# Retention stage of a two-layer transformer kernel: all four score groups at once, a chunk pipeline one step deeper, and GpSimd weighting the gathered expert rows

## The reference

```python
# end of layer 0: each token adds its two experts' rows, weighted
weighted = fc2 * padded_probs[:, None]
moe_out = jnp.zeros((N, H)).at[padded_tid].add(weighted)
x = h1 + moe_out
# layer 1, retention: 8 sequences of 512 tokens, 16 heads of 16
y = layernorm(x)
Q, K, V = y @ WQ, y @ WK, y @ WV          # per head
Q, K = xpos_rotate(Q), xpos_rotate(K)
R = ((Q @ K^T) * decay_mask) @ V          # causal, one decay per head
x = x + group_norm(R, gamma, beta) @ WO
```

## Time and profile before

| | us |
|---|---|
| median of three runs | 2053.84 (2051.27 to 2053.95) |
| the profiled execution | 2054.74 |
| its span, from the first to the last instruction | 2053.0 |
| retention stage in it | about 1425 to 1780 |

### The profile page before, as it was taken

How to read it: one execution, slowest core, us unless ns; L and a number is a source line. 1 busy time by engine, 2 the same in 40 slices (tenths; PEclk the granted TensorE clock), 3 DMA queues, 4 the chain that set the end, 5 groups by cost and what they waited for, 6 DMA issues and landing times. The chain is left out here.

```text
span 2053.0 us, 33292 instructions
## 1 busy us (share of the span) xinstructions
PE 1724.3 (84%) x10092; PEld 1280.7 (62%) x10092; DVE 1209.3 (59%) x3206; ACT 667.7 (33%) x2056; POOL 583.1 (28%) x668
## 2 busy tenths in 40 slices
PE   4767766999899967267857999996899999799998
PEld 2444435777677744156756888885566666456655
DVE  5999994777677765799843221222677777422221
ACT  2545554554455424012320111111344444211111
POOL 2434432000000011787516333332344443200000
PEclk9998987999999989678865999998999999799999
DMA  6000000000000000000022324222000000000000
GB/s 184 19 13 15 15 18 11 11 11 12 13 11 12 1 9 0 6 3 21 34 95 67 93 85 110 92 86 98 27 27 26 26 26 26 1 11 20 10 20 21
DMA packets 55111, 71.08 MB, mean 35 GB/s; under 512 B 7074, under 2 KB 44898, under 8 KB 54626
## 3 DMA queue, kind: packets, MB, share of 16 engines
q1 hardware_dynamic: 37218, 40.46, 6.3%
q0 software_dynamic: 6912, 18.88, 3.6%
q10 hardware_dynamic: 10880, 10.49, 1.5%
HBM read 46.61 MB, written 23.20 MB: 34 GB/s over the span
## 5 line engine op out<-in xcount | busy, mean ns | idle before, releaser
L801 ACT ACTIVATE probs<-psS,nm 128x256 f32<-128x256 f32 x256 | 118.9, 469 | 189.5 <-DVE nm L834 189.5
L409 PE MATMUL psKV<-wkv,XT 128*128 128x512 f32 x256 | 135.8, 679 | 52.2 <-DVE acc L545 32.5
L1576 DVE COPY YE<-e_psY 128x512 f32<-128x512 f32 x40 | 27.7, 691 | 220.6 <-PE e_psY L1522 220.6
L545 DVE SCALAR_TENSOR_TENSOR acc<-psKV,G,acc 128x128 f32<-128x128 f32 x544 | 150.2, 333 | 6.7 <-ACT gated L470 6.7
L1512 PE MATMUL e_psH<-e_XT,w 128*128 128x256 f32 x640 | 147.1, 384 | 0.0
L1522 PE MATMUL e_psY<-w,e_HT 128*128 128x256 f32 x640 | 144.0, 379 | 0.0
L832 DVE TENSOR_REDUCE mx<-psS 128x2 f32<-128x512 f32 x128 | 87.9, 686 | 90.9 <-PE psS L722 90.9
L722 PE MATMUL psS<-Rec,QT 128*128 128x256 f32 (+1 forms) x512 | 133.7, 384 | 5.4 <-issue 4.5
L1482 POOL DMA_INDIRECT XE<-token_rows,held x80 | 76.0, 950 | 200.2 <-PE e_psX L1499 180.5
L1522 PEld LDWEIGHTS e_psY<-w,e_HT 128*128 128x128 f32 x640 | 121.6, 190 | 16.5
L1512 PEld LDWEIGHTS e_psH<-e_XT,w 128*128 128x128 f32 x640 | 120.6, 193 | 15.4
(11 more groups left out here) (254 smaller groups left out, 3872.0 us busy)
## 6 DMA issues: line engine op xcount, KB each, us to landing
expert_out<-YE ACTq DMA_DIRECT2D x40, 256.0 KB, 2.2
w<-in_w SPq DMA_DIRECT2D x16, 512.0 KB, 4.3
X<-in_x SPq DMA_DIRECT2D x8, 512.0 KB, 7.6
x_turned<-XT SPq DMA_DIRECT2D x32, 128.0 KB, 2.1
XS<-x_turned SPq DMA_DIRECT2D x8, 512.0 KB, 4.0
token_rows<-o_XN SPq DMA_DIRECT2D x32, 128.0 KB, 1.7
out_x<-X SPq DMA_DIRECT2D x8, 512.0 KB, 2.9
QT<-in_sel SPq DMA_DIRECT2D x2, 1024.0 KB, 11.5
```

Source lines behind the costliest of these rows:

```text
L409: mm = pe.matmul(psKV[v % 2][half][:, :, :], XT[:, v, c, :], wkv[:, c, half * 512:(half + 1) * 512], start=(c == 0), stop=(c == KC - 1))
L545: ins = nc.vector.scalar_tensor_tensor(acc[:, v % 2, e, :], kv, g, acc[:, v % 2, e, :], ALU.mult, ALU.add)
L801: nc.scalar.activation(probs[:, b.q % 4, hg, :], psS[b.q % 2][:, hg, :], ACT.Exp, bias=nm[:, b.q % 2, hg:hg + 1], scale=scale, accum_out=s ...
```

## The change

It leaves every stage but `retention` as it is. In `retention`:

- **Scores** are one piece: all four groups of 32 rows at once, into four banks of PSUM (`psS[r]`) where there were two. To make room, `psX` and `psV` share a bank (`psXV`), `psR`, the state's `psNew` and the turned inverses share one (`psRS`), and the variances go to `psQK`. Waits are added for that: to_state waits for result_read, variances for rotate of the entering chunk, inverses_turned for the state, project_v for the next chunk's x_turned.
- **The pipeline** has one more step: a step enters g, scores g-1, takes from_chunk, to_state, squared and variances of g-2, and lets g-3 leave. The rows of g+3 are gathered, those of g+2 are added and take their statistics, and g+1 is normalised and transposed. Steps -3 to 34 run where -2 to 33 did.
- **The expert rows** of a chunk are weighted and summed on GpSimd (`arrived` there: one multiply of 512 columns, one add of 256), behind the gather of the next chunk; VectorE adds only their sum to `X`.
- **Copies by parity** of V are a piece of their own on ScalarE (`values_parted`), read from `V` in SBUF.

```diff
--- before.py
+++ after.py
...
         cidx = k.sb(ctx, "cidx", [P, 2, 2], U32)
+        weight = k.sb(ctx, "weight", [P, 2, 2])
+        rows = k.sb(ctx, "n_rows", [P, 2, D])
...
-        psT = k.ps(ctx, "n_psT", [P, 2, KC, P])
+        psXV = k.ps(ctx, "n_psXV", [P, 2, D])
         psQK = k.ps(ctx, "n_psQK", [P, 2 * D])
-        psV = k.ps(ctx, "n_psV", [P, 2 * D])[:, 0:D]
         psK = k.ps(ctx, "n_psK", [P, 2, KC, P])
-        psX = k.ps(ctx, "n_psX", [P, 2, KC, P])
-        psVar, psInv = psX[:, 0, 0, 0:H1], psX[:, 1, :, :]
-        psS = [k.ps(ctx, f"n_psS{s}", [P, KC, 2, P]) for s in range(2)]
-        psR = k.ps(ctx, "n_psR", [P, 2, KC, P])[:, 0, :, :]
+        psRS = k.ps(ctx, "n_psRS", [P, 2, KC, P])
+        psS = [k.ps(ctx, f"n_psS{r}", [P, KC, 2, P]) for r in range(4)]
+        psX, psV = psXV[:, 0, :].rearrange("p (c t) -> p c t", c=KC), psXV[:, 1, :]
+        psR, psNew = psRS[:, 0, :, :], psRS[:, 1, :, :]
+        psInv, psVar = psR, psQK[:, 0:H1]
...
-            for g in range(-2, TS):
...
             with eng.Fori(1, NB - 1) as i:
                 for s in range(TS):
                     step(i, s, lambda d: True)
-            for g in range(NT - TS, NT + 2):
+            for g in range(NT - TS, NT + 3):
...
+        class Chunk:
+            def __init__(self, i, s, lag):
+                w = s + lag
+                self.g, self.i, self.s, self.x = i * TS + w, i + w // TS, w % TS, w % 2
+                self.pair = i * (TS // 2) + w // 2
+                self.states = self.i * (TS - 1) + self.s
+                self.adds = self.i * (TS - 2) + max(self.s - 1, 0)
+                self.ends = self.s == TS - 1
...
+            def turn_x(c):
+                pe.wait_ge(xn_ready, c.g + 1 + 2)
+                pe.wait_ge(z_added, c.g)
+                pe.wait_ge(v_evac, c.g)
...
+            def project_v(c):
+                pe.wait_ge(xt_evac, upto(c.g + 2))
+                pe.wait_ge(z_added, c.g + 1)
...
-            def scores(g, half):
-                if half == 0:
...
+            def scores(c):
+                pe.wait_ge(x_evac, c.g * 2 + 4)
+                pe.wait_ge(s_masked, c.g * 4 + 4)
+                for h in range(KC):
                     for par in range(2):
                         for r in range(4):
...
+            def to_state(c):
+                pe.wait_ge(r_read, c.g + 2)
...
+            def variances(c):
+                pe.wait_ge(sq_ready, c.g + 1)
+                pe.wait_ge(rot_done, upto(c.g + 3) + 1)
...
+            def inverses_turned(c):
+                pe.wait_ge(inv_spread, c.g + 1)
+                pe.wait_ge(st_done, c.g + 3)
...
             def step(i, s, has):
-                g, entering, attending, leaving = i * TS + s, has(0), has(-1), has(-2)
-                if attending:
-                    scores(g - 1, 0)
-                if leaving:
-                    variances(g - 2)
-                if entering:
-                    turn_x(g, s)
-                if attending:
-                    from_state(g - 1)
-                if entering:
-                    project_qk(g)
-                if leaving:
-                    inverses_turned(g - 2)
-                if entering:
-                    project_v(g)
-                if attending:
-                    scores(g - 1, 1)
-                if leaving:
-                    out(g - 2, entering)
-                if entering:
-                    turn_qk(g, s)
-                if attending:
-                    from_chunk(g - 1, s)
-                if attending and s != 0:
-                    to_state(s)
+                new, one, two, three = Chunk(i, s, 0), Chunk(i, s, -1), Chunk(i, s, -2), Chunk(i, s, -3)
+                if has(-3):
+                    inverses_turned(three)
+                if has(0):
+                    project_qk(new)
+                if has(-3):
+                    out(three)
+                if has(-2):
+                    from_state(two)
+                    from_chunk(two)
+                if has(-1):
+                    scores(one)
+                if has(-2):
+                    if not two.ends:
+                        to_state(two)
+                    variances(two)
+                if has(1):
+                    turn_x(Chunk(i, s, 1))
+                if has(0):
+                    turn_qk(new)
+                    project_v(new)
...
             def step(i, s, has):
-                g, entering, attending, leaving = i * TS + s, has(0), has(-1), has(-2)
-                if leaving:
-                    root_of(g - 2)
-                if entering:
-                    x_turned(g)
-                if leaving:
-                    inverse_spread(g - 2)
-                    scaled(g - 2)
-                if entering:
-                    values(g, s)
+                new, one, two, three = Chunk(i, s, 0), Chunk(i, s, -1), Chunk(i, s, -2), Chunk(i, s, -3)
+                if has(-3):
+                    scaled(three)
+                if has(-1):
+                    queries_turned(one)
+                    values_parted(one)
+                if has(2):
+                    deviation(Chunk(i, s, 2))
+                if has(-2):
+                    result_read(two)
+                    root_of(two)
                 if has(1):
-                    deviation(g + 1, (s + 1) % 2)
-                if entering:
-                    qk_turned(g)
-                if attending:
-                    result_read(g - 1, s)
+                    x_turned(Chunk(i, s, 1))
+                if has(-2):
+                    inverse_spread(two)
+                if has(0):
+                    keys_turned(new)
+                    values(new)
             stream(act, step)
...
-            def gathered(g, x, i):
-                pool.wait_ge(rows_used, g + 1)
-                nc.gpsimd.tensor_copy(cidx[:, x, :], k.slots[:, bass.ds(g, 1), :].rearrange("p a j -> p (a j)")).then_inc(i_ready, 1)
-                pool.wait_ge(i_ready, g + 1)
...
+            def gathered(c):
+                pool.wait_ge(first_added, c.g - 1) if not isinstance(c.g, int) or c.g > 1 else None
+                nc.gpsimd.tensor_copy(cidx[:, c.x, :], row(k.slots, c.g)).then_inc(i_ready, 1)
+                nc.gpsimd.tensor_copy(weight[:, c.x, :], row(k.prob, c.g)).then_inc(i_ready, 1)
+                pool.wait_ge(i_ready, c.g * 2 + 2)
                 pass_gate(k, pool)
                 for j in range(2):
-                    pool.indirect_dma_start(YG[:, x, j, :], None, k.y_dram[:, :],
-                                            bass.IndirectOffsetOnAxis(ap=cidx[:, x, j:j + 1], axis=0)).then_inc(got[x], 16)
...
+            def arrived(c):
+                pool.wait_ge(got[c.x], c.pair * 32 + 32)
+                pool.wait_ge(rows_used, c.g + 1)
+                nc.gpsimd.tensor_tensor(YG[:, c.x, :, :], YG[:, c.x, :, :], bc(weight[:, c.x, :].unsqueeze(2), [P, 2, D]),
+                                        ALU.mult).then_inc(weighed, 1)
+                pool.wait_ge(weighed, c.g + 1)
+                nc.gpsimd.tensor_tensor(rows[:, c.x, :], YG[:, c.x, 0, :], YG[:, c.x, 1, :], ALU.add).then_inc(first_added, 1)
...
             def step(i, s, has):
-                g, entering, attending, leaving = i * TS + s, has(0), has(-1), has(-2)
+                if has(3):
+                    gathered(Chunk(i, s, 3))
                 if has(2):
-                    gathered(g + 2, s % 2, i)
-                if entering:
-                    rotated(g, s)
-                if attending:
-                    squared(g - 1, s)
+                    arrived(Chunk(i, s, 2))
+                if has(0):
+                    rotated(Chunk(i, s, 0))
+                if has(-2):
+                    squared(Chunk(i, s, -2))
...
-            def arrived(g, x, pair, j):
-                if j == 0:
-                    dve.wait_ge(got[x], pair * 32 + 32)
-                else:
-                    dve.wait_ge(first_added, g + 1)
-                ins = nc.vector.scalar_tensor_tensor(row(k.X, g), YG[:, x, j, :], row(k.prob, g)[:, j:j + 1], row(k.X, g),
-                                                     ALU.mult, ALU.add)
-                ins.then_inc(rows_used if j else first_added, 1)
...
+            def arrived(c):
+                dve.wait_ge(first_added, c.g + 1)
...
+                nc.vector.tensor_tensor(row(k.X, c.g), row(k.X, c.g), rows[:, c.x, :], ALU.add).then_inc(rows_used, 1)
...
             def step(i, s, has):
-                g, entering, attending, leaving = i * TS + s, has(0), has(-1), has(-2)
-                if attending:
-                    mask(g - 1, 0)
-                if leaving:
-                    inverses(g - 2)
+                new, one, two, three = Chunk(i, s, 0), Chunk(i, s, -1), Chunk(i, s, -2), Chunk(i, s, -3)
+                if has(-2):
+                    mask(two, 2)
+                if has(-3):
+                    result(three)
+                if has(-2):
+                    mask(two, 3)
```

(30 more changed lines are left out.)

293 lines of the change are left out of this document (141 added, 152 removed).

## The result

| | us |
|---|---|
| kernel before, median of four runs | 2053.86 (2051.27 to 2053.95) |
| changed kernel, median of four runs | 2069.63 (2066.63 to 2072.90) |
| ratio, with its 95% interval | 1.0080 (1.0061 to 1.0099) |
| profiled execution of the changed kernel, and its span | 2071.33, 2069.2 |

The account below looks back on a forecast made before the run. TensorE was taken as the bound before, a ring through ScalarE and VectorE of 10.25 us a step after; 4.4 for filling, -3.8 for the middle and 4.7 for emptying add 5.3 us to 2054.74: 2060, range 2044 to 2079.

Parts of the forecast that it names:

- The ring: Retention step: ScalarE's deviation of g+2, awaiting VectorE's statistics, precedes the result read of g-2; a closed chain of 10.24 us.
- Step by step the sums: Running totals from one Q/K projection: VectorE starts, 1.92; rotate, 3.18; norm, 4.71; deviation starts, 6.19; variances, 7.67; project_v, 9.06; next projection, 10.24.
- The rival with the looser ring: Retention loop: result read does not wait for statistics, TensorE's order bounds at about 8.6 us; 2017 us, chance 0.08.
- the other loose ring: Retention loop: a ring of 9.5 to 9.9 us, for rows that hid waits; 2035 to 2047 us, chance 0.08.
- Scores hidden: TensorE's scores in one pass take about 1.1 us instead of 2.3; the 1.2 us saved only becomes TensorE idle time.
- GpSimd covered: GpSimd's new multiply and add, 2.1 us, end some 1.7 us before VectorE asks for the sum, costing nothing.
- The rule in the Trainium skill: Elementwise tile work belongs on VectorE, GpSimd being about twice as slow: 1.1 us a step, 35 us, so 2095.
- Filling and emptying: Retention's start and end: first projection 4.4 us later, and 4.7 us more from the last projection to the last statistics.
- The middle: Retention, first to last Q/K projection: 311.3 us against 315.1, so 3.8 us earlier.
- 8.1 + 6.9 + 9.3 + 28 x 10.25: First to last Q/K projection: three filling steps of 8.1, 6.9 and 9.3 us, then 28 full steps of 10.25; 311.3 us.
- The clock was a rival at 0.07: TensorE idling 1.6 to 2.3 us before the variances loses clock: 1.7 us in seven steps, 2072; chance 0.07.
- my 2060: Whole kernel: the forecast time, 5.3 us more than the profiled 2054.74, 0.3% slower; own case chance 0.70.

Follow-up runs that it names:

- e1: Changed kernel with ScalarE's result read of g-2 moved ahead of the deviation of g+2; 2019.01 us, ratio 0.9832 to the kernel before.
- e5b: Order of e1, with the scores issued as two halves of two row groups, back to back; 2022.37 us, ratio 0.9851 to the kernel before.
- e11: Changed kernel with the expert rows back on VectorE and the scores issued three times; 2084.85 us, ratio 1.0147 to the kernel before.
- e6: Changed kernel with the scores issued twice into the same banks, in TensorE's idle time; 2060.11 us, ratio 1.0036 to the kernel before.
- e3: Order of e1, with the expert rows weighted and added on VectorE again; 2042.90 us, ratio 0.9946 to the kernel before.
- e4: Kernel before, old pipeline and scores, with only the weighting and sum of the expert rows moved to GpSimd; 2061.15 us, ratio 1.0043.
- e5a: Changed kernel, in its own order, with the scores issued as two halves of two row groups; 2073.92 us, ratio 1.0096 to the kernel before.
- e2: Changed kernel, in its own order, with the expert rows back on VectorE as two fused multiply-adds; 2127.96 us, ratio 1.0374 to the kernel before.

## Why the prediction came out as it did

- **The ring: right.** ScalarE waits about 4 us at the deviation (4.02), and the result read follows it 2.2 us after its product. Step by step the sums were 3.18, 4.71, 6.19, 7.67, 9.06 and 10.24. The timeline has 3.19 (1604.86 - 1601.67), 4.83, 6.21, 7.51, 8.85 and 10.03. I had 10.25 for a full step, and steps at full clock take 10.14. e1 shows it by taking the ring away.
- **The rival with the looser ring**, "TensorE's own order is the bound at about 8.6 us" and 2017 us, describes e1 well: 8.84 and 2019. The bound there is VectorE's chain, though, not TensorE's order, since e5b gives TensorE 0.55 us more a step, 17 us in 31, and costs 3 us in all; but TensorE has only some 0.6 us a step to spare there, so the two bounds lie close together. The range of the other loose ring was added up wrongly: 9.5 to 9.9 in 28 steps gives 2039 to 2050 by its own terms, not 2035 to 2047.
- **Scores hidden: right.** One pass takes 1.17 (1.1 forecast) and buys TensorE idle time alone.
- **GpSimd covered: right.** Its sum is done at 1602.89, 3.6 us before VectorE adds it, and the group of that add shows no wait. The two operations took 1.85 from start to end, inside 1.8 to 2.2; the multiply took 1.05, and the 1.47 of the earlier trace rows was no good guide to it. The rule in the Trainium skill, GPSIMD Engine Reference, section 4.1 Engine selection, would have put the kernel at 2095. As to the price of one operation the trace agrees (0.73 against 0.41). As to the kernel it doesn't: against the rows on VectorE the move saves 24 us in the order of e1 and 58 in the change's, of which 25 are left when TensorE is kept busy (e11 against e6).
- **Filling and emptying: right in size.** 3.6 for 4.4 (3.0 with the shorter stages ahead), and 5.3 for 4.7.
- **The middle failed**: forecast 3.8 us shorter, measured 8.9 longer. Two terms of "8.1 + 6.9 + 9.3 + 28 x 10.25" did it. The first three intervals took 30.2, not 24.3; through the first, and for 2 us of the second, the clock was still low (1424 to 1454 in the window above). In the kernel before it was up some 13 us earlier, but for one fall of 3.4 us. In the third there was a fall of 3.4 us too. How much of these 5.9 is the clock and how much the order was not separated. The other term is the 28 steps: 293.9 for 287. 21 full steps were 0.11 shorter than forecast, the last was 2.0 shorter, and six with a low clock were 12.0 us longer.
- **The clock was a rival at 0.07**, with 1.7 us in seven steps and 2072. It came as described: six steps, 2.0 us each, and 2069.6. It failed only by its chance. I put that low because gaps of 1.62 us had kept the clock in another stage. That inference was the wrong step. e6 shows that the falls cost some 10 us. That e6 lies at my 2060 (2060.11) is in part luck: its stage took 362.5 us from GpSimd's first copy to the last statistics where my sum gives 358.5, and the other stages happened to be 4.7 shorter than in the kernel before.

What stays open is when exactly the clock falls. In the changed kernel the same gap stands before the variances in every fourth step, once with a fall and once without:

```profile
1585.03 1.03 PE L1810 MATMUL n_psQK<-group,n_sq 128*128 128x16 f32 x4 [2.47 <-POOL n_sq L1970]
...
1670.41 0.61 PE L1810 MATMUL n_psQK<-group,n_sq 128*128 128x16 f32 x4 [2.47 <-POOL n_sq L1970]
```

The same instructions took 1.03 us at the lower clock and 0.61 at the full one.

The deeper pipeline wasn't tried by itself. By differences, in the order of e1, GpSimd's part is worth 24 of the 35 us (e3), the one-pass scores 3 (e5b), and the other 8 are left for the pipeline and the other edits. These shares hold for this order alone: in the kernel before, GpSimd's part costs 7.5 (e4).

## What to carry to other kernels

Before you shorten an engine's work, look at what stands ahead of the critical piece in the queue of each helper engine: here one small square root, placed ahead of a copy that TensorE waits for, cost 50 us, 12 of them through the clock. That is more than the 35 us that the change gains without it. When a change makes the busiest engine idle in short pieces, count its clock as part of the price: TensorE, waiting 1.5 us in every step, also ran slower here. Work moved to GpSimd was free here only where it had time to spare and its tile operations didn't meet VectorE operations on two SBUF tiles; look for a VectorE group whose mean rose.

## What the runs showed of the hardware

- **VectorE stands still behind GpSimd.** An operation with both inputs in SBUF that starts while GpSimd works on a tile is longer: 1.27 for 0.43 (e4, ten of ten), 0.83 for 0.41 (e1), 1.46 for 1.10 (e3). In e4 and e1 it ends 0.28 us after GpSimd's. An operation with one input in PSUM kept its 0.42 beside GpSimd's multiply or add (n_RN in the changed kernel, 19 of 19). It goes the other way too: where VectorE came first in e1, GpSimd's square took 0.84 instead of 0.61. The Trainium skill, SBUF — State Buffer, section SBUF: two separate sides, calls it an exclusive lock: whichever starts first holds the ports for the whole instruction. These runs agree in the main; but 0.28 is less than the 0.41 to 0.43 that the operation takes alone, so a part of it ran before GpSimd's recorded end. And the norm, with one tile in SBUF, took 0.54 for 0.41 behind GpSimd's Kr in the changed kernel (19 of 19); why is open. In the changed kernel the add of the sum kept its 0.41, by the luck of its place; in e1 the mean of its group is 0.735, and it lies on the ring. Moving the square out of its way, worth up to 10 us (31 steps of 0.32), was not tried.
- **The clock can fall with gaps of 1.5 to 2.5 us that come back every step**, at TensorE 83% busy. With gaps of 1.0 to 1.1 in three steps of four and 1.9 in the fourth it fell as often (e5a); with 0.6 to 0.7 and 1.6 it fell once (e6). With 2.2 to 3.1 in each step it was at the lower level so often that the window shows 0.80 (e2).
- **Four row groups of 32 run side by side**: 32 records in 1.17 us, where two groups at a time take 1.16 for 16 and 1.72 for 32 back to back (e5a).
